# A one-core transformer layer with routed experts: sums copied to the output eleven tiles before the end, and a reordered way into the tiles

## The reference, cut to what matters

```python
h = token_select(x)                       # x (16, 4, 128, 256): 4 groups weighted into one, h (16, 128, 256)
h = h + attention(layernorm(h))           # 16 heads, relative bias, 128 tokens per image
n = layernorm(h)
gates = softmax(n @ Wg + bg)              # 8 experts, the best 2 kept and normalised
e_out = gelu(n @ W1[e] + b1[e]) @ W2[e] + b2[e]
out = h + sum over the two experts of gate * e_out      # (16, 128, 256)
```

## Time and profile before

| | us |
|---|---|
| median of 3 runs | 566.88 (564.5 to 567.76) |
| profiled execution | 565.29 |
| its span on the core | 563.5 |
| PE busy with matmuls | 510.7 (91%) |
| DVE, ACT, POOL busy | 239.5, 265.3, 200.2 |
| PE's share of the chain that ended last | 60% |

### The profile page before, as it was taken

One profiled execution on the slowest core, in us unless ns is written; L12 is line 12 of the kernel. 1 busy time (PEld: TensorE's weight loads), 2 busy tenths in 40 slices (PEclk: granted clock), 3 DMA queues, 4 the chain that ended last, 5 costly groups with the idle time before them and its releaser, 6 DMA issues.

```text
span 563.5 us, 13115 instructions
## 1 busy us (share of the span) xinstructions
PE 510.7 (91%) x3742; PEld 418.9 (74%) x3743; DVE 239.5 (42%) x1083; ACT 265.3 (47%) x1003; POOL 200.2 (36%) x186
## 2 busy tenths in 40 slices
PE   4789899999999989938999999999999999999980
PEld 3466666666666657617998999999999989999960
DVE  2777787888787887822233111111111111111110
ACT  1267688777887878743343333332233223333310
POOL 3041133334544455311326653333333333333221
PEclk9999899999999999978999999999999999999995
DMA  8890020303131221284566666666666666666615
GB/s 264 253 332 6 20 95 21 95 20 95 35 100 23 92 50 65 73 294 118 169 184 184 165 161 161 185 180 182 185 186 185 186 184 178 167 183 166 158 19 158
DMA packets 51004, 78.61 MB, mean 139 GB/s; under 512 B 10528, under 2 KB 39472, under 8 KB 50768
## 3 DMA queue, kind: packets, MB, share of 16 engines
q1 hardware_dynamic: 40160, 66.80, 36.6%
q0 software_dynamic: 8592, 10.58, 11.1%
q10 hardware_dynamic: 2208, 0.71, 0.6%
HBM read 68.27 MB, written 11.90 MB: 142 GB/s over the span
## 4 chain that ended last, share of the span: by engine, by line
PE 60%; DVE 10%; issue 10%; DMA 8%; ACT 6%; POOL 3%; POOLq 0%; SPq 0%; DVEq 0%; ACTq 0%
PE psVO L956 20%; PE psS L944 10%; PE psP L944 10%; ACT prob L586 5%; DMA fold<-xn_dram,sel 5%; PE psQK L782 4%; PE psS L805 3%; DVE prob L1122 3%; PE psP L815 3%; PE psVO L793 2%; PE psVO L836 2%; PE psQK L932 2%; DMA meta_dram<-meta,pos 1%; DMA sel<-meta_dram 1%; DVE st L1080 1%
## 5 line engine op out<-in xcount | busy, mean ns | idle before, releaser
L956 PE MATMUL psVO<-xw,prob 128*128 x624 | 142.0, 380 | 0.8 <-DVE fold L1348 0.8
L956 PEld LDWEIGHTS psVO<-xw,prob 128*128 128x128 f32 x624 | 115.5, 190 | 16.0 <-issue 1.2
L485 POOL DMA_INDIRECT sum_dram<-fold,sel x39 | 62.0, 1590 | 166.8 <-DMA sel<-meta_dram 125.2
L586 ACT ACTIVATE prob<-prob,smin 128x128 f32<-128x128 f32 x256 | 99.5, 395 | 15.0 <-DVE smin L1122 14.8
L672 ACT ACTIVATE prob<-psS,b1T 128x128 f32<-128x128 f32 x160 | 45.6, 368 | 99.6 <-PE psS L944 99.5
L672 ACT ACTIVATE prob<-psP,b1T 128x128 f32<-128x128 f32 x152 | 43.3, 368 | 95.6 <-PE psP L944 95.6
L428 POOL TENSOR_TENSOR rstd<-ve,minus_half 128x1 f32<-128x1 f32 x32 | 33.2, 1037 | 144.9 <-DVE ve L1085 139.2
L944 PEld LDWEIGHTS psS<-fold,w1c 128*128 128x128 f32 x640 | 75.8, 195 | 1.9 <-DVE fold L1343 1.0
L944 PE MATMUL psS<-fold,w1c 128*128 128x128 f32 x640 | 76.3, 278 | 0.6 <-DVE fold L1343 0.6
L944 PEld LDWEIGHTS psP<-fold,w1c 128*128 128x128 f32 x608 | 70.7, 192 | 3.0 <-DVE fold L1343 2.1
L944 PE MATMUL psP<-fold,w1c 128*128 128x128 f32 x608 | 71.1, 275 | 1.9 <-DVE fold L1343 1.9
(11 more groups left out here) (165 smaller groups left out, 535.6 us busy)
## 6 DMA issues: line engine op xcount, KB each, us to landing
w1c<-in_L_ffn_W SPq DMA_DIRECT2D x39, 1024.0 KB, 6.7
xw<-in_x SPq DMA_DIRECT2D x16, 512.0 KB, 8.1
xw<-in_L_ffn_W SPq DMA_DIRECT2D x8, 1024.0 KB, 6.7
sum_dram<-h_all SPq DMA_DIRECT2D x17, 128.0 KB, 2.5
xn_dram<-xn SPq DMA_DIRECT2D x16, 128.0 KB, 1.7
out<-sum_dram SPq DMA_DIRECT2D x4, 512.0 KB, 5.6
relb<-in_L_ffn_b SPq DMA_DIRECT2D x1, 1024.0 KB, 6.7
sel<-meta_dram SPq DMA_DIRECT2D x39, 2.0 KB
```

The source lines that it names most:

```text
L485: pool.indirect_dma_start(out=sum_dram.ap()[0:EARLY_B * S if j < EARLY else N_TOK + P, :], out_offset=bass.IndirectOffsetOnAxis(ap=row_no[ ...
L586: i = act.activation(blk, blk, ACT.Exp, bias=smin[:, k:k + 1], scale=-1.0, accum_out=ssum[:, k:k + 1])
L956: i = pe.matmul(psVO[:, 0:D], hT[u][:, c * P:(c + 1) * P], xw2[:, bass.ds(e * (HC * D) + c * D, D)], start=(c == 0), stop=(c == HC - 1))
```

## The change

It has five pieces.

1. **The sums.** The 25 late tiles are split into 14 middle ones (`MID`, which hold what isn't certain to be full) and 11 last ones (`LAST`), which are certainly full, so that they touch no dummy row. SP waits for the scatters of tiles 0 to 27, copies `sum_dram` to `out` after it has issued W1 of tile 31, and goes on with the records of tile 33. The last 11 scatters accumulate into `out`; the first of them, `scatter(28)`, waits for the four copies. POOL's list leaves out a scatter at `j` = 31, so that `gather(32)` comes before `scatter(28)`. The end waits for the last scatter alone.
2. **Two buffers `yout`.** DVE waits for the scatter before the last one; POOL waits for the last one to land before it issues the next.
3. **The tables.** The second table becomes `late_counts`, `middle_table` and `last_table`, done by DVE behind the results of tiles 3, 4 and 5.
4. **The way into the tiles.** SP issues W1 of tiles 0 and 1 as soon as the early table is there, ahead of the last `xn2` stores and of the records, and b2 after the records of tiles 0 and 1. PE transposes tile 1 before it projects the last image; DVE copies tile 1 out before it does that image's residual.
5. **The image steps.** On PE the values of head groups 0 and 1 stand together, and those of 2 and 3 behind the second scores. On DVE the reciprocals of the softmax sums (`srcp`, `srcw`) come ahead of the first norm.

```diff
-LATE = TILES - EARLY
+LAST = -(-(SLOTS - E * (P - 1)) // P) - EARLY
+MID = TILES - EARLY - LAST
+TABLE = max(EARLY, MID, LAST)
...
-        yout = fold[:, 3 * D:4 * D]
+        yout = [fold[:, 3 * D:4 * D], sel[:, 0:D]]
...
+            with sp.Fori(0, E - 2) as e:
+                load_w2(e)
+                for u in range(2):
+                    store_xn2(2 * e + u)
+            load_w2(E - 2)
+            store_xn2(B - 4)
+            load_w2(E - 1)
+            sp.wait_ge(tables_ok, 1)
+            load_w1(0, 0)
+            load_w1(1, 1)
+            store_xn2(B - 3)
+            sp.dma_start(sum_dram.ap()[N_TOK:N_TOK + P, :], hcol(0)).then_inc(h_out, 16)
+            sp.wait_ge(scat, 16 * TOPK * EARLY_B)
             load_records(0)
-            load_w1(0, 0)
             next_records(1)
-            load_w1(1, 1)
+            sp.wait_ge(s_min, NCH * B)
+            sp.dma_start(relb[:, 0:E * D], b2.rearrange("e d -> (e d)").partition_broadcast(P)) \
+                .then_inc(b2_in, 16)
             next_records(2)
...
-            with sp.Fori(EARLY // 2, TILES // 2) as t:
+            with sp.Fori(EARLY // 2, (EARLY + MID) // 2 + 2) as t:
+                for u in range(2):
+                    next_records(2 * t + (u + 1))
+                    load_w1(2 * t + u, u)
+            out_v = out.rearrange("b p d -> (b p) d")
+            rows_ = N_TOK // 4
+            sp.wait_ge(y_scat, 16 * (EARLY + MID))
+            for i in range(4):
+                sp.dma_start(out_v[i * rows_:(i + 1) * rows_, :],
+                             sum_dram.ap()[i * rows_:(i + 1) * rows_, :]).then_inc(fin_out, 16)
+            with sp.Fori((EARLY + MID) // 2 + 2, TILES // 2) as t:
...
             load_w1(TILES - 1, 0)
+            sp.wait_ge(fin_out, 16 * 4)
             sp.wait_ge(y_scat, 16 * TILES)
...
                 pool.wait_ge(y_sb, j + 2)
+                if j > 0:
+                    pool.wait_ge(y_scat, 16 * j)
+                if j == EARLY + MID:
+                    pool.wait_ge(fin_out, 16 * 4)
                 own_wait(pool)
                 pool.indirect_dma_start(
-                    out=sum_dram.ap()[0:EARLY_B * S if j < EARLY else N_TOK + P, :],
+                    out=sum_dram.ap()[0:EARLY_B * S if j < EARLY else N_TOK + P, :] if j < EARLY + MID
+                    else out.rearrange("b p d -> (b p) d"),
                     out_offset=bass.IndirectOffsetOnAxis(ap=row_no[:, j * META + 2:j * META + 3], axis=0),
-                    in_=yout, in_offset=None, compute_op=ALU.add).then_inc(y_scat, 16)
+                    in_=yout[j % 2], in_offset=None, compute_op=ALU.add).then_inc(y_scat, 16)
...
                 gather(j)
-                scatter(j - 3)
+                if j < EARLY + MID + 3:
+                    scatter(j - 3)
+                elif j > EARLY + MID + 3:
+                    scatter(j - 4)
...
                     values(i - 1, 0)
+                    values(i - 1, 1)
                     context(i - 1, 1 - u, 2)
-                    values(i - 1, 1)
                 if front:
                     scores(i, 0)
                 if back:
                     context(i - 1, 1 - u, 3)
                     spread_sums(i - 1)
-                    values(i - 1, 2)
                 if front:
                     scores(i, 1)
                 if back:
+                    values(i - 1, 2)
                     values(i - 1, 3)
...
             hidden(0, 0, 0)
+            turn_xs(1, 1, 0)
             out_project(B - 1)
-            turn_xs(1, 1, 0)
...
+                if back:
+                    reciprocals(i - 1, 1 - u)
+                    spread(i - 1)
                 if nxt:
                     first_norm(i + 1)
                 if place is not None:
                     rows(place)
-                if back:
-                    reciprocals(i - 1, 1 - u)
-                if back:
-                    spread(i - 1)
...
+            def early_tables():
+
+                tile_counts(c_t[:, :], 0)
+                tile_table(0, EARLY, c_t[:, :])
+                dve.sem_inc(tables_ok, 1)
+
+            def late_counts():
+
+                tile_counts(c_t[:, :], 0)
+                then(dve.tensor_tensor(c_t[:, :], c_t[:, :], taken[:, 0:E], ALU.subtract))
+                tile_ends(c_t[:, :])
+                tiles_taken(c_last, c_t[:, :], LAST)
+                then(dve.tensor_tensor(taken_too[:, 0:E], taken[:, 0:E], c_last, ALU.add))
+                tile_counts(c_all, P - 1)
+                then(dve.tensor_tensor(c_all, c_all, taken_too[:, 0:E], ALU.subtract))
+
+            def middle_table():
+
+                tile_table(EARLY, MID, c_all, taken_too)
+                dve.sem_inc(tables_ok, 1)
+
+            def last_table():
+
+                tile_table(EARLY + MID, LAST, c_last, taken)
+                dve.sem_inc(tables_ok, 1)
+
+            dve.wait_ge(gp_late, 5)
+            early_tables()
...
-                if not (isinstance(j, int) and j == 0):
-                    dve.wait_ge(y_scat, 16 * j)
-                dve.tensor_scalar(yout, ysum, metas[:, bass.ds(j * META + 1, 1)], None, ALU.mult) \
+                if not (isinstance(j, int) and j <= 1):
+                    dve.wait_ge(y_scat, 16 * (j - 1))
+                dve.tensor_scalar(yout[u], ysum, metas[:, bass.ds(j * META + 1, 1)], None, ALU.mult) \
...
-            residual(B - 1)
             top_index(B - 2, slot(B - 2))
             xs_evac(1)
+            residual(B - 1)
             second_norm(B - 1)
             xs_evac(2)
-            result(0, expert(0))
+            dve.wait_ge(b2_in, 16)
+            result(0, 0, expert(0))
...
+            late_counts()
             xs_evac(6)
-            result(4, expert(4))
+            result(4, 0, expert(4))
+            middle_table()
             xs_evac(7)
-            result(5, expert(5))
+            result(5, 1, expert(5))
+            last_table()
+            dve.wait_ge(tables_ok, 3)
```

108 lines of the change are left out of this document (47 added, 61 removed).

## The result

The changed kernel takes 557.88 us, the median of 4 runs (555.63 to 558.88), beside 566.38 for the kernel before (564.5 to 567.76): ratio 0.9859, 95% interval 0.9829 to 0.9889. It is faster by 1.4%, 8.5 us; 15.3 were forecast, and the time lies above the range. The profiled execution took 557.26, with a span of 554.3. Executions over 1.5% above the fastest of their kernel are left out of the ratios in this document: among the changed kernels one, of 562.81 (e1_catchup), and one of 1807.93 of the kernel before beside it.

A forecast was written before the change was run, and what follows sets the result against it. PE bounds the tiles; gains lie where it stands still, on the way in and in the tail. 565.3 - 9.8 - 5.3 + 0.3 - 0.5 = 550.0 profiled, 551.6 by the median, stated as 551; range 546.5 to 555.5.

The forecast's parts named there:

- the end of the tail: After the last scatter's issue: 3.8 us to land plus 0.35, span ending at 553.7 for 563.5, a gain of 9.8.
- the image steps: Reordered PE values and DVE reciprocals: 0.25 us at most in each of three rank steps, 0 in ordinary steps; -0.5 in all.
- the last scatter: At the tail, POOL's last scatter was to be issued at 549.48 instead of 549.80.
- Later scatters follow each other at about 4 us and catch up within 7.2 us a tile: After scatter 28 waits for the copies, POOL's following scatters, spaced by their landing, were to recover the delay.
- The copies in the tiles: Copies of the sums, issued from 476.9 on and landed by 487.4, hidden in the tiles: cost 0.
- Rival C: Copies run at half rate beside W1 and gathers in the tiles, landing at 493.5: 556 us; chance 0.08.
- The threshold of 488.5: For the copies in the tiles: each us by which they land after 488.5 costs one us.
- The way in: Between image steps and tiles: first gather lands 3.4 us sooner, a 1.9 us wait for DVE goes; -5.3 in all.
- rival B: The way into the tiles gains little, record scatter and gather as slow as now: 554 us; chance 0.14.
- The tables: Splitting the second table and adding waits on the early table and POOL's scatters: +0.3 us.
- Rival F: In ten ordinary image steps DVE's first norm holds POOL's power, 0.3 us each: 554 us; chance 0.08.
- The exclusive lock: Skill's rule that DVE and POOL share a port pair, locked for a whole instruction by whoever starts first.

The follow-up runs named there:

- e1_catchup: Changed kernel with POOL issuing one scatter more at tile 34, so three instead of four are left for the end; ratio to the kernel before 0.9775.
- e2: Changed kernel with POOL waiting for the last scatter's landing before its program ends; ratio to the kernel before 0.9885.
- e3: Changed kernel plus a 1 KB copy on SP behind the last landing, with a wait; ratio to the kernel before 0.9796.
- e4: Changed kernel with the four copies at the end again, all scatters into the sums, POOL scattering three tiles back throughout; ratio to the kernel before 0.9891.
- e9: Changed kernel with SP's list around the way into the tiles in the old order; median 556.85 us, ratio to the kernel before 0.984.
- e6: Changed kernel, unchanged, profiled again; ratio to the kernel before 0.9841, image steps 0 to 14 in 187.6 us.
- e5: Kernel before, unchanged, profiled again; image steps 0 to 14 in 188.6 us.
- e11: Changed kernel, unchanged, in another set of runs; ratio to the kernel before 0.9806, image steps 0 to 14 in 184.9 us.
- e12: Kernel before, unchanged, in another set of runs; image steps 0 to 14 in 188.3 us.
- e15: Changed kernel with DVE's reciprocals behind the first norm and the rows again; image steps 0 to 14 in 186.0 us.
- e8: Changed kernel with DVE's reciprocals behind the first norm and the rows again; ratio to the kernel before 0.9828, image steps 0 to 14 in 187.2 us.
- e16: Changed kernel with POOL's last gather ahead of the scatters of tiles 33 and 34; tail 24.4 us.
- e18: Changed kernel, unchanged, in another set of runs; median 557.27 us, ratio to the kernel before 0.983.

## Why the prediction was wrong

**The step that failed is the end of the tail**, "Landing 3.8 later, 553.3, and 0.35: the end is at 553.7". It takes the time behind SP's last wait (0.35) as all that remains once the copies are gone. The span was to end within 0.5 us of the last landing and ended some 5 behind it. What ends it is POOL's closing, 8.8 us from the issue of its last scatter, where the step has 3.8 + 0.35: e2 moves the end with that closing, and e3 shows that SP's own last wait doesn't set it. In the kernel before, POOL had until 558.4 to close, unseen under copies that ran until 563.2. Gone with the copies is only what stuck out: 4.4 us on average, 5.0 with e4. I asked for every stall what is late next, and here not: POOL's last work, an instruction or in e2 a wait, ends 7.0 us ahead of its program's end in every profile. Predicted from this, the last step gives 549.48 + 8.8 = 558.3 for 563.5, and the sum 554.6, 556.2 by the median. That is inside the medians measured in the second kind (555.65 to 557.88). Part of this agreement is luck: the terms for the image steps and for the last scatter were wrong too, as follows.

**"Later scatters follow each other at about 4 us and catch up within 7.2 us a tile"** held in 7 of 13 profiles. The landing of 3.8 was right for scatters as they stood before, with the load 1.8 us behind them or none. But the copies push scatter 28 back by 11.6 us, and from there the scatters can fall 0.6 us ahead of the loads, where they take 6.1 to 7.9. Price: 1.6 us where it fails, and some 0.4 to 0.7 at tile 38; on average the last scatter came 0.3 later than before, where 0.3 sooner was forecast.

**The copies in the tiles**: right for PE. They went out at 470.83 (476.9 at the latest was forecast), landed in 7.8 (within 11), and PE shows no idle time in tiles 31 to 34 of the first profile. Rival C didn't come. The threshold of 488.5 doesn't follow from the working around it, which with the slow gather of 6.23 leaves POOL no slack beyond 487.4; with the copies 6 us sooner it wasn't tested.

**The way in**: right in size, -5.0 for -5.3. By the means of the profiles the first hidden layer comes 3.0 sooner (3.4 forecast, 3.3 by its own numbers, 252.5 less 249.2; SP's order alone is 3.9 by e9) and the second another 1.9 (1.9 forecast). Within it the gather was priced too low: PE starts 6.2 us behind its issue in the first profile, where 4.8 and little more were taken, and the first layer took 5.80 for 5.24. By its length alone that gather is the sign named for rival B; but it was issued 2.2 us sooner (244.07 for 246.29). **The tables**: +0.5 over the tiles for +0.3, within the gather waits of single executions (272.1 to 274.1). Rival B, with 1.9 and 0.5 for the whole, fell.

**The image steps**: the -0.5 comes near the measured -0.9 in the second kind by luck. The forecast left out steps 1 and 2, where the edits give 1.5, and had the rank steps faster, where they cost 0.7 in all (e6 beside e5). In the first kind it is 2.8 us short of the measured -3.3. The value pairs, for which 0.25 in a rank step was the most, gave 0.3 to 0.8 in each in the first kind, and the earlier trace rows had their wait of 1.10 in full view; of steps 1 and 2 I had read no row. Rival F fell: ordinary steps stay at 12.6. It expected the norm to start ahead of the power; in fact the power starts first and the norm 0.19 us behind it, and neither holds the other: 0.63 for the power (0.65 before) and 0.40 for the norm (0.68 before, beside POOL's product). The exclusive lock that the prediction named with this rival isn't seen for this pair.

The result lies outside the range since the range took the copies' price as known. A bound for that price was in the trace of before: the last end of any engine's closing, 558.37.

## What to carry to other kernels

Work taken off the very end shortens a kernel only down to what it hid. Before pricing it, look for each engine at what follows its last instruction up to the end of its program, and put the end at the latest of them. In this kernel that is the end of POOL's last DMA instruction plus 7 us, so the thing to bring forward is POOL's last instruction; a 1 KB transfer of SP behind it was free. A queue written out by hand that loses a slot gets it back only if its waits are shorter than the period while the other traffic runs, so price a landing where the large load beside it is issued at the same distance as it will be after the change. And profile the two kernels in more than one set of runs before reading a difference of 2 us.

## What the runs showed of the hardware

- The closing of POOL took 7.0 us from the end of its last work in all 20 profiles (8.79 with the last DMA instruction in it in 19, 7.01 in e2); PE's took 2.84, ACT's 0.81, DVE's 0.37 to 0.40. The Trainium skill ("Runtime: NRT & Kernel Launch", The ~15µs preamble/postamble breakdown) gives the closing barrier about 1.5 us. An estimate by that figure would have put some 1.5 in place of the prediction's 0.35; here some 5 us passed behind the last landing, and the measurement decides.
- Scatters that accumulate landed in 3.6 to 3.9 us with no 1 MB load issued near them, in 3.5 to 4.4 when one was issued 1.4 to 2.0 us behind them, and in 6.1 to 7.9 when it was 0.3 to 1.0 us behind. Adding into `out` (3.6 to 3.9 at the end) cost no more than into `sum_dram` (3.7 to 3.9 in e4).
- A rank step as the changed kernel has it took 13.0 to 13.1 us in three sets of runs (e1 to e4, e9 to e11, e12 to e15) and 13.8 to 14.1 in the first profile and two other sets (e5 to e8, e16 to e18), where PE's semaphore event for a value product came up to 1.8 us behind the last matmul. The kernel before took 13.3 to 13.9 in both kinds, and medians of 565 to 566 us.
